# A decoder layer with mixture of experts: loops written out, gate and up products split into high and low parts, router sums interleaved

## The reference

```
x = x + attn_stack(layernorm(x))        # 8 layers of linear attention + MLP, 16 heads of 64, hidden 1024
x = x + cross_attention(layernorm(x))   # 16 heads of 16
x = x + ffn(layernorm(x))               # shared expert + one of 8 experts for each token

# ffn, for the 2048 tokens z (256 wide), hidden 512:
swiglu(z, wg, wu, wd) = silu(z @ wg.T) * (z @ wu.T) @ wd.T
logits = z @ gate_w.T;  top = argmax(logits);  score = sigmoid(max(logits))
out = swiglu(z, shared) + swiglu(z * score, expert[top])
```

## Time and profile before

| | |
|---|---|
| median of 3 runs | 3004.3 us (3002.4 to 3007.04) |
| profiled execution | 3003.99 us, its span 3002.3 us |
| TensorE busy | 2851.9 us, 95% of the span |
| VectorE busy | 2353.7 us, 78% |
| ScalarE busy | 1867.5 us, 62% |
| GpSimd busy | 777.2 us, 26% |
| mean granted TensorE clock | 0.975 of full speed |
| instructions | 37724 |
| attention stack and cross attention, route, experts | 0 to 2721, to 2853, to 3002 us of the span |

### The profile page before, as it was taken

One profiled execution on the slowest core, in us unless ns is written; L12 is line 12 of the kernel. 1 busy time (PEld: TensorE's weight loads), 2 busy tenths in 40 slices (PEclk: granted clock), 3 DMA queues, 4 the chain that ended last, 5 costly groups with the idle time before them and its releaser, 6 DMA issues. The chain is left out here.

```text
span 3002.3 us, 37724 instructions
## 1 busy us (share of the span) xinstructions
PE 2851.9 (95%) x12878; PEld 2307.5 (77%) x12879; DVE 2353.7 (78%) x3523; ACT 1867.5 (62%) x2797; POOL 777.2 (26%) x514
## 2 busy tenths in 40 slices
PE   5899999999999999999999999999999986996999
PEld 4688888788878887888788878887888875775555
DVE  7878898889888988898889888988898836773111
ACT  5667777777777777777777777677767733441122
POOL 4003231323132313231323132313231124332122
PEclk8899999999999999999999999999999998996999
DMA  4000000000000000100000000000100016000121
GB/s 139 1 1 27 31 19 21 28 31 18 22 28 31 18 22 28 31 18 22 28 31 18 22 28 31 18 22 28 31 18 6 1 56 232 0 0 4 47 46 30
DMA packets 62501, 92.35 MB, mean 31 GB/s; under 512 B 16480, under 2 KB 42336, under 8 KB 60256
## 3 DMA queue, kind: packets, MB, share of 16 engines
q1 hardware_dynamic: 58224, 85.55, 9.0%
q0 software_dynamic: 4080, 4.34, 0.8%
HBM read 80.24 MB, written 10.54 MB: 30 GB/s over the span
## 5 line engine op out<-in xcount | busy, mean ns | idle before, releaser
L407 PE MATMUL PS<-XTHI,WHI 128*128 128x512 f32 x1536 | 624.7, 407 | 32.7 <-DVE EX L733 19.7
L409 PE MATMUL PS<-XTHI,WLO 128*128 128x512 f32 x1536 | 606.9, 395 | 0.0
L408 PE MATMUL PS<-XTLO,WHI 128*128 128x512 f32 x1536 | 602.9, 393 | 0.0
L618 ACT ACTIVATE ATT<-INV,CC,CE 128x128 f32<-128x128 f32 x1024 | 432.4, 485 | 124.1 <-PE Y L449 117.9
L449 PE MATMUL Y<-WO,ATT 128*128 128x256 f32 x2048 | 455.9, 381 | 5.8 <-ACT ATT L618 5.8
L449 PE MATMUL Y<-W2S,H 128*128 128x256 f32 x2048 | 457.5, 379 | 2.3 <-DVE T L805 1.4
L449 PEld LDWEIGHTS Y<-WO,ATT 128*128 128x128 f32 x2048 | 390.7, 191 | 62.7 <-ACT ATT L618 5.3
L449 PEld LDWEIGHTS Y<-W2S,H 128*128 128x128 f32 x2048 | 386.2, 190 | 56.3 <-DVE T L805 1.8
L407 PEld LDWEIGHTS PS<-XTHI,WHI 128*128 128x128 f32 x1536 | 291.0, 189 | 100.3 <-issue 32.5
L323 POOL TENSOR_TENSOR RSTD<-MV,EPS 128x4 f32<-128x4 f32 x68 | 16.1, 237 | 1357.2 <-DVE MV L820 1348.7
L583 ACT ACTIVATE EX<-PS,BNEG 128x512 f32<-128x512 f32 x256 | 165.7, 685 | 299.9 <-DVE INV L785 158.1
(11 more groups left out here) (187 smaller groups left out, 4679.9 us busy)
## 6 DMA issues: line engine op xcount, KB each, us to landing
STAGE<-L_attn_Wkvq SPq DMA_DIRECT2D x64, 384.0 KB, 3.1
WO<-L_attn_Wo SPq DMA_DIRECT2D x8, 1024.0 KB, 4.8
W2S<-L_attn_W SPq DMA_DIRECT2D x8, 1024.0 KB, 5.1
STAGE<-L_attn_W SPq DMA_DIRECT2D x32, 256.0 KB, 4.9
WGU<-L_ffn_r_gate SPq DMA_DIRECT2D x8, 512.0 KB, 9.3
WGU<-L_ffn_r_up SPq DMA_DIRECT2D x8, 512.0 KB, 9.1
WD<-L_ffn_r_down SPq DMA_DIRECT2D x8, 512.0 KB, 9.2
rows_in<-ZERO SPq DMA_DIRECT2D x1, 3128.0 KB, 16.0
```

Of the source, the lines that this page charges most:

```text
L407: nc.tensor.matmul(out, whi[:, kc, :], xhi[:, kc, :], start=(kc == 0), stop=False)
L408: nc.tensor.matmul(out, whi[:, kc, :], xlo[:, kc, :], start=False, stop=False)
L409: ins = nc.tensor.matmul(out, wlo[:, kc, :], xhi[:, kc, :], start=False, stop=(kc == KD - 1))
L618: ins = nc.scalar.activation(ATT[:, 2 * p + i, ss], INV[:, b, i, ss], ACT.Identity, scale=CE[:, b, k:k + 1], bias=CC[:, b, k:k + 1])
```

## The change

1. The loops over the layers of the attention stack (five streams) and over the pairs of expert blocks (all streams that had one) become Python loops: every iteration is written out, with the layer number and all waits as constants.
2. The shared expert's gate and up products become three fp32r matmuls each. ScalarE makes the high parts (SGUHI, ZGHI), VectorE the low ones (SGULO, ZGLO): SGU once, each of the four token tiles once.
3. The router's sums on VectorE are no longer one chain: `gated(0,0)` and `gated(0,1)` come behind OH, `gated(0,2)` behind the BASE sums, `gated(0,3)` behind EID.
4. The experts' gate and up products become three fp32r matmuls each. For each block ScalarE copies the chosen expert's gate and up weights (128x1024 each) to EHI, VectorE subtracts for ELO; both now read the expert number with `value_load`. The turned input is split too (XTUHI by ScalarE, XTULO by VectorE).
5. To make room, small tiles move into the space of EX, STAGE and ZERO, a row of `rows_in` has 264 instead of 272 values, and the memset of BASE moves from GpSimd to VectorE.

```
-            with pe.Fori(0, LAYERS - 1, 1) as l:          # the same in sp, pool, act, dve
+            for l in range(LAYERS - 1):
...
-ROW_W = D + 16
+ROW_W = D + 8
...
             def gate_up(q, c):                            # route, TensorE
                 n = q * FC + c
+                if c == 0:
+                    pe.wait_ge(zg_lo, q + 1)
+                if n == 0:
+                    pe.wait_ge(sgu_lo, 2)
                 for m, (done, read) in enumerate(((g_mm, sg), (u_mm, hs))):
                     if n >= 2:
                         pe.wait_ge(read, n - 1)
+                    out = PSX[:, 2 + 2 * (c % 2) + m, :]
                     for kc in range(KD):
-                        ins = nc.tensor.matmul(PSX[:, 2 + 2 * (c % 2) + m, :], SGU[:, m, kc, c * P:(c + 1) * P],
-                                               ZG[:, q, kc, :], start=(kc == 0), stop=(kc == KD - 1))
+                        hi, lo = (w[:, m, kc, c * P:(c + 1) * P] for w in (SGUHI, SGULO))
+                        nc.tensor.matmul(out, hi, ZGHI[:, q % 2, kc, :], start=(kc == 0), stop=False)
+                        nc.tensor.matmul(out, hi, ZGLO[:, q % 2, kc, :], start=False, stop=False)
+                        ins = nc.tensor.matmul(out, lo, ZGHI[:, q % 2, kc, :], start=False, stop=(kc == KD - 1))
...
+            def high(q):                                  # route, ScalarE
+                act.wait_ge(zg, q + 1)
+                if q >= 2:
+                    act.wait_ge(u_mm, (q - 1) * FC)
+                nc.scalar.copy(ZGHI[:, q % 2, :, :], ZG[:, q, :, :]).then_inc(zg_hi, 1)
+            for m in range(2):
+                nc.scalar.copy(SGUHI[:, m, :, :], SGU[:, m, :, :]).then_inc(sgu_hi, 1)
...
                 nc.scalar.activation(SGS[:, c % 2, :], PSX[:, 2 + 2 * (c % 2), :], ACT.Silu).then_inc(sg, 1)
+                if c == 0 and 0 < n // FC < TILES - 1:
+                    high(n // FC + 1)
...
+            def low(q):                                   # route, VectorE
+                dve.wait_ge(zg_hi, q + 1)
+                nc.vector.tensor_tensor(ZGLO[:, q % 2, :, :], ZG[:, q, :, :], ZGHI[:, q % 2, :, :].bitcast(F32),
+                                        ALU.subtract).then_inc(zg_lo, 1)
...
             nc.vector.tensor_tensor(OH[:, :, :], IOTE[:, :, :], spread(IDX[:, :], E), ALU.is_equal).then_inc(oh, 1)
+            gated(0, 0)
+            gated(0, 1)
             dve.wait_ge(pre_mm, 1)
...
             for b in range(SEQS):
                 then(nc.vector.tensor_tensor(BASE[:, b + 1, :], BASE[:, b, :], TOTS[:, b, :], ALU.add))
+            gated(0, 2)
...
             then(nc.vector.tensor_scalar(EID[:, :], EIDF[:, :], float(E - 1), None, ALU.min))
+            gated(0, 3)
...
+            def high(i, j, m):                            # experts, ScalarE
+                u = 2 * i + j
+                if not (type(i) is int and i == 0):
+                    act.wait_ge((g_mm, u_mm)[m], u - 1)
+                e = nc.scalar.value_load(EID[0:1, bass.ds(u, 1)], min_val=0, max_val=E - 1)
+                nc.scalar.copy(EHI[:, j, m, :, :], WGU[:, e, m, :, :]).then_inc(e_hi, 1)
...
             def pair(i, more):                            # experts, ScalarE
                 evac_hidden(i, 0)
                 silu(i, 1)
-                evac_input(i + 1, 0)
+                if more:
+                    high(i + 1, 1, 0)
+                input_hi(i + 1, 0)
+                if more:
+                    high(i + 1, 1, 1)
                 evac_hidden(i, 1)
                 silu(i + 1, 0)
                 if more:
-                    evac_input(i + 1, 1)
+                    high(i + 2, 0, 0)
+                    input_hi(i + 1, 1)
+                    high(i + 2, 0, 1)
...
+            def low(i, j, m):                             # experts, VectorE
+                u = 2 * i + j
+                dve.wait_ge(e_hi, 2 * u + (m + 1))
+                e = nc.vector.value_load(EID[0:1, bass.ds(u, 1)], min_val=0, max_val=E - 1)
+                nc.vector.tensor_tensor(ELO[:, j, m, :, :], WGU[:, e, m, :, :], EHI[:, j, m, :, :].bitcast(F32),
+                                        ALU.subtract).then_inc(e_lo, 1)
...
             def pair(i, first, more):                     # experts, VectorE
                 product(i, 1)
+                input_lo(i + 1, 0)
+                if more:
+                    low(i + 1, 1, 0)
+                    low(i + 1, 1, 1)
                 result(i, 0, first)
                 product(i + 1, 0)
+                if more:
+                    input_lo(i + 1, 1)
+                    low(i + 2, 0, 0)
+                    low(i + 2, 0, 1)
                 result(i, 1, first)
```

More of the change, by code:

```diff
@@ L392, in _ @@
             slot(0, 1)
-            with pool.Fori(0, LAYERS - 1, 1) as l:
+            for l in range(LAYERS - 1):
                 for t in range(2, TILES + 2):
@@ L711, in _ @@
             slot(0, 1)
-            with act.Fori(0, LAYERS - 1, 1) as l:
+            for l in range(LAYERS - 1):
                 for t in range(2, TILES + 2):
@@ L927, in _ @@
             slot(0, 1)
-            with dve.Fori(0, LAYERS - 1, 1) as l:
+            for l in range(LAYERS - 1):
                 for t in range(2, TILES + 2):
@@ L1306, in mixture, with route @@
         PSX = ctx.enter_context(nc.psum_tensor("PSX", [P, 8, 512], F32))
-        route(nc, X, ident, cross.rows, ffn, EID, ROW, PSX, out)
-        experts(nc, ident, ffn, EID, PSX, out)
-def route(nc, X, ident, ZN, ffn, EID, ROW, PSX, out):
+        route(nc, X, ident, cross, cross.rows, ffn, EID, ROW, PSX, out)
+        experts(nc, ident, cross, ffn, EID, PSX, out)
+def route(nc, X, ident, cross, ZN, ffn, EID, ROW, PSX, out):
     with ExitStack() as ctx:
@@ new lines, in route, with behind_rows @@
+        ex = cross.EX[:, :, :, :].rearrange("p b i t -> p (b i t)")
+        stage = cross.STAGE[:, :, :].rearrange("p s n -> p (s n)")
+        def behind_rows(first, n, a):
+            first += SEQS * ROW_W
+            return ex[:, first:first + n].rearrange("p (x a) -> p x a", a=a)
+        SGS = behind_rows(0, 2 * TOK, TOK)
+        LG, PICK, OH, TOTS, POS, IOTE = (behind_rows(2 * TOK + k * P, P, E) for k in range(6))
+        IOT128 = behind_rows(2 * TOK + 6 * P, P, SEQS)
+        BASE = behind_rows(2 * TOK, (SEQS + 1) * E, E)
@@ L1560, in added, with experts @@
                 ins.then_inc(upd, 1)
-            for q in range(TILES):
+            for q in range(1, TILES):
                 for c in range(FC):
                     gated(q, c)
-                    if c == 0 and q > 0:
+                    if c == 0:
                         added(q - 1)
+                    if c == 1 and q + 1 < TILES:
+                        low(q + 1)
             added(TILES - 1)
-def experts(nc, ident, ffn, EID, PSX, out):
+def experts(nc, ident, cross, ffn, EID, PSX, out):
     with ExitStack() as ctx:
@@ L1606, in _ @@
                          ).then_inc(token_in, 16)
-            with sp.Fori(1, PAIRS, 1) as i:
+            for i in range(1, PAIRS):
                 for j in range(2):
@@ L1639, in gate_up @@
                 u = 2 * i + j
-                e = nc.tensor.value_load(EID[0:1, bass.ds(u, 1)], min_val=0, max_val=E - 1)
-                pe.wait_ge(xt, u + 1)
+                pe.wait_ge(xt_lo, u + 1)
                 for m, done in enumerate((g_mm, u_mm)):
@@ L1685, in _ @@
             pair(0, True)
-            with pe.Fori(1, PAIRS - 1, 1) as i:
+            for i in range(1, PAIRS - 1):
                 pair(i, True)
```

127 lines of the change are left out of this document (77 added, 50 removed).

## The result

The changed kernel takes 2965.48 us (median of 4 runs, 2964.72 to 2966.76); the kernel before, run beside it, 3004.12 (3002.4 to 3007.04). The ratio is 0.987, with a 95% interval of 0.9858 to 0.9881: 38.6 us faster, where 46.0 were forecast. The profiled execution took 2964.72 us with a span of 2962.1, against a span of 3002.3 before: 40.2 us to account for.

What follows compares the result with a forecast made beforehand. TensorE, busy for 95% of the span, was taken as the bound. Loops -8.2, shared expert -22.0 and experts -15.8 sum to -46.0, from 3004.0 to 2958.0 us; range 2950 to 2984.

Steps and rivals of the forecast that it cites:

- likeliest case: Whole kernel: all terms as forecast, with small exposures, 2951 to 2965 us; chance 0.55.
- The loops: Attention layers: writing the loops out removes TensorE's six "issue" waits at the jumps back, -8.2 us.
- Rival 3: Layer loops written out give nothing (2966 us; chance 0.06) or cost time (0.04, shared with rivals together over 46 us).
- The products: Shared expert: fp32r matmuls at 0.229 us; the stretch falls from 98.2 to 76.2 us, -22.0, half products, half stalls.
- The sums' chain: Shared expert: TensorE's 7.35 us wait behind VectorE's router sums and 1.7 us of half clock go, leaving 0.4 us.
- The scatter's stall: Shared expert: TensorE's wait of 1.49 us, while ScalarE and VectorE stand during the scatter, was taken as gone.
- rival 2: Shared expert: the scatter's stall comes into the open, 14.8 us plus 2 of half clock, total 2975 us; chance 0.15.
- The start of the experts: Before the experts' blocks: the input's low part adds 0.3 to 0.4 us, first products give back 0.6; weight conversions covered.
- The experts: Expert blocks: each falls from 5.82 to 5.13 us with TensorE still the bound, 23 blocks, -15.8 us.
- Both prices: Expert blocks: `value_load` (0 to 0.8 us) mostly covered; POOL's indirect DMA beside VectorE's subtraction (0 to 1.0 us) taken as 0.
- the 2962 us that hung on it: Expert blocks: if indirect DMAs conflict with VectorE's two-input subtractions, 5.3 us a block and 2962 us in total.
- Rival 1: Expert blocks: the conversions bind VectorE, 5.7 to 6.7 us a block, total 2971 to 2994 us; chance 0.2.

Runs made afterwards that it cites:

- loops alone: The kernel before with only its loops over layers and over pairs of expert blocks written out: 2994.22 us, ratio 0.997.
- second trace: Profile of the unedited changed kernel, run once more later beside its variants: 2960.44 us, ratio 0.9858.
- sums alone: The kernel before with only the router's sums placed between the shared products; f32 products and hardware loops kept: 2993.45 us, ratio 0.9968.
- products alone: The changed kernel with the layer loops and the order of the router's sums put back as before: 2985.47 us, ratio 0.9944.
- first set: Four kernels on one chip: loops only, sums only, products only, and one scatter DMA of 16; the kernel before took 3003.47 us there.
- paced: The changed kernel with the scatter's 16 indirect DMAs issued in four groups of four, each after a tile's HS: 2959.78 us, ratio 0.9853.
- late scatter: The changed kernel with the whole scatter held back until two tiles' HS are done: 2960.26 us, ratio 0.9856.
- no-scatter kernel: The changed kernel with only the first of the scatter's 16 indirect DMAs: 2959.77 us, ratio 0.9855.
- the input first: The changed kernel with the scatter in four groups and the experts' input split ahead of weights due later: 2957.99 us, ratio 0.9849.
- one load and the input first: The changed kernel with grouped scatter, input split early, and one `value_load` a block on ScalarE and VectorE: 2958.34 us, ratio 0.9853.
- third set: Later runs on another chip: the unedited changed kernel (2960.44 us) beside three variants; the kernel before took 3002.88 us there.

## Why the prediction was right, and where its terms were off

**The result against the range.** The mechanisms named for the three big terms are the ones that the runs show, but that the first result lies in the range owes something to its width: 2965.48 is half a microsecond outside the likeliest case's own range (2951 to 2965), and inside the stated one (2950 to 2984) because that made room for the rivals. The same kernel without the stall, 2960.44, lies inside both.

**The loops** (-8.2 forecast; -9.25 alone, 1.6 us a layer). Right in place and mechanism: the "issue" waits were those of the jump back, and the written-out code brought no others. Code is fetched less, not more: 1.59 + 0.56 = 2.15 MB over the run, against 2.46. The Trainium skill (Advanced Engine Details and Errata, ISA Cache) gives an engine two cache lines of 256 instructions, and TensorE more. The body is longer, 1346 matmuls and as many weight loads on TensorE, and in these runs TensorE stops at the jump back and nowhere in the straight code; whether the stop is a fetch or the jump itself, no run tells apart. Rival 3 is refuted. The layers gave 8.7 us up to the first shared product in the kernel with the loops alone, 9.6 and 9.8 in the two traces of the changed kernel, so 0.5 to 1.6 more than the forecast.

**The products.** The chunks ran at 0.229 us a matmul, as taken from the earlier trace rows. In the execution without the stall the shared stretch takes 77.0 us where 76.2 were added up, -21.2 against -22.0.

**The sums' chain.** The step was right: TensorE's 7.35 us of idle time and the half clock behind it went. Its remainder was 1.0 us in place of 0.4 (0.83 in the second trace), so the term is mis-sized by some 0.5 us: the 16 sums of BASE took 3.92 us in the changed kernel, and 3.18 in the kernel with the sums alone.

**The scatter's stall** (taken as gone; rival 2 had it at 14.8 + 2 us). This is the term that was off in the result: 3.91 us of idle time and 1.7 of half clock. Rival 2 named the place, the engines and the way in which TensorE would meet it, and the end: 2796.3 in the times of before is 2786.5 in the changed kernel, which runs 9.8 us ahead, and there ScalarE starts again (2786.55). It had the size wrong: the two engines didn't stand through to that end, but three times for 2 to 6.5 us, and only VectorE's 5 us in the middle came into the open; the last stand lay under the down. What the traces say of the stall and its cause:
- Of the three kernels that have the sums in one piece (before, loops alone, products alone) all three show idle time of 13.7 to 16.3 us on ScalarE and VectorE at the same chunk. Most of it is no stall, since a down lies in it that VectorE has to wait for: VectorE starts 5.9, 5.1 and 7.4 us after the end of that down, where it starts 0.1 us after it in the tiles without a stall. In all four traces that have a stall its end comes 1.8 to 2.6 us after POOL has issued the last indirect DMA.
- Of the eleven traces with the sums between the chunks only one shows a stall of more than 1 us, the first of the changed kernel, and the same kernel ran again without it.
- So by count the stall goes with the old order of the sums, and on the chip of the first set both orders ran with the whole scatter, the old one twice with the stall and the new one once without. The gain of "sums alone" (10.0) holds the 1.49 us that it cost. No run shows why, and the order isn't the whole of it. The scatter is there in each trace that has a stall; but as the unedited kernel could run without one, the kernels with less, paced and late scatter prove nothing. The 5.7 us between the no-scatter kernel and the result are not shown to be the scatter's price: the changed kernel was 5.0 us faster with the scatter in place.
- What makes the two engines late was not found. Whether TensorE had really signalled in time can't be read from a wait that is labelled "remote". Open too is whether the kernel before has its stall in each execution: there is one trace of it, and on TensorE it cost 1.49 us.

**The start of the experts** (+0.35 - 0.6 forecast, +1.4 measured). The step that failed was "conversions of the first weights lie beside the load of XU". ScalarE begins them 3.6 us after the last down, with 1.6 us of that load left, and VectorE when it is over, each with a `value_load` in front that nothing covers; then VectorE does two subtractions before the input's low part. In the kernel without `value_load` the copies begin 2.1 us after the last down, and the first two subtractions do end before XU is there. To the first product it is 1 us less without `value_load`, 1.2 less with the input first (0.9 of it lost again in the second block), and 1.8 less with one load and the input first.

**The experts** (-15.8 forecast, -16.3 and -15.1 in the two traces, 5.13 us a block forecast and measured). Both prices that the trace of before didn't show were 0, as taken. `value_load` leaves gaps of 0.3 us on VectorE and ScalarE, within their slack. Subtractions took 1.22 us also where they met POOL's indirect DMAs; but in the experts they overlap by 0.54 us at most, so a block could hardly have shown the price, and it is the ZGLO of the route, 0.91 us beside the scatter, that shows it as 0. By the rule of the Trainium skill (Advanced Engine Details and Errata, GPSIMD Details) that I had weighed, an instruction with two SBUF inputs conflicts with POOL; beside an indirect DMA, which computes no tensor, these rows don't show it, and the 2962 us that hung on it don't hold. Rival 1 is refuted.

**The sum.** -9.6 for the layers, -21.2, +1.4 and -15.1 give the 44.5 us by which the span of the changed kernel's second trace is shorter, against the 46.0 of the forecast. The first trace has 4.3 less: 5.7 for the stall, with 1.2 given back by the clock in the experts and 0.1 in the layers. The time on record, 2958.0, is 7.5 us below the result and 2.4 below the same kernel in the third set.

## What to carry to other kernels

A long chain of small sums on an engine that also feeds TensorE is best cut at the feeding instructions: 10 us came from moving four calls. When products get cheaper, look at what ends just behind them, as the waits that they covered come into the open (7.35 to 8.71 us, 1.49 to 4.04). Before an edit is held to have removed a stall, run the unedited kernel beside it: here the stall was gone without an edit. And idle time in front of an instruction is not all stall: take off what the same instruction waits for in a tile or an execution without one.

## What the runs showed of the hardware that was not expected

- A jump back at the end of a body of 1346 matmuls costs TensorE 1.1 to 1.6 us of idle time and the layer 1.6 us in the mean; written out, the same code runs without that stop.
- While POOL issued 16 indirect DMAs of a scatter, ScalarE and VectorE started instructions 5 to 7 us later than the TensorE work in front of them explains, in four traces of fourteen, and in one of two of the same kernel. TensorE lost 0.7 to 4.0 us by it. No engine's work in the trace accounts for it.
- Three fp32r matmuls of 512 columns for one f32 product take 0.69 us in place of 0.857, and an engine that splits the operands at 1.05 and 1.22 us a tile of 1024 keeps up with it.
- A subtraction of VectorE with two SBUF inputs kept its 1.22 us with 0.91 of them beside POOL's indirect DMAs; beside POOL's arithmetic such an instruction took up to 3.2 us in place of 1.23.
- In the cross attention, the same code in each kernel, the granted clock fell for two stretches more in one execution than in that of the kernel before, and cost 3.3 us.
- The clock's rise after the idle time ahead of the experts came after 6 matmuls in one execution and after 12 in another of the same kernel: 1.2 us that no edit explains.
